# Layer 0 attention: keys on partitions for the probabilities, maxima from a first score product

## The reference, cut to what matters

```
y_dca, y_main = y[:, -DCA:, :], y[:, :-DCA, :]          # DCA = 16
q = _ln((x @ Wq + bq).reshape(b, s1, H, HD), qn_w, qn_b)
k, v             = ... of y_main @ Wk + bk, y_main @ Wv + bv ; k = _ln(k, kn_w, kn_b)
k_dca, v_dca     = ... of y_dca @ Wkv_dca + bkv_dca     ; k_dca = _ln(...)
ctx     = softmax(q k^T * SCALE) v
ctx_dca = softmax(q k_dca^T * SCALE) v_dca
return (ctx + ctx_dca) @ Wo + bo
```

## Time and profile before

| what | us |
|---|---|
| median of three runs | 2358.55 |
| the profiled execution | 2357.19 |
| its span in the trace | 2355.4 |
| projection stage | 7 to 101.6 |
| attention stage | 101.6 to 294.8 |
| output product | 295.0 to 310 |

### The profile page before, as it was taken

One profiled execution on the slowest core, in us unless ns is written; L12 is line 12 of the kernel. 1 busy time (PEld: TensorE's weight loads), 2 busy tenths in 40 slices (PEclk: granted clock), 3 DMA queues, 4 the chain that ended last, 5 costly groups with the idle time before them and its releaser, 6 DMA issues. The chain is left out here.

```text
span 2355.4 us, 42854 instructions
## 1 busy us (share of the span) xinstructions
PE 2082.5 (88%) x12471; PEld 1729.0 (73%) x12471; DVE 1555.0 (66%) x4480; ACT 1226.4 (52%) x3030; POOL 760.3 (32%) x1130
## 2 busy tenths in 40 slices
PE   5698879799999995799999878888769999997999
PEld 3454468577999992588888767777658999986887
DVE  6699857756878884788888752111246877885665
ACT  3799933656666661566666412222216666653333
POOL 3443310202333320323332166666622333311221
PEclk9799989899999997899999888999889999997999
DMA  2157020102211204000000137776750000004331
GB/s 63 37 111 204 1 90 1 67 7 88 74 56 67 73 19 146 5 1 0 0 0 1 45 101 202 212 209 194 210 177 21 21 20 13 20 2 127 110 109 52
DMA packets 132900, 174.04 MB, mean 74 GB/s; under 512 B 43868, under 2 KB 99140, under 8 KB 130088
## 3 DMA queue, kind: packets, MB, share of 16 engines
q1 hardware_dynamic: 121704, 140.27, 20.5%
q0 software_dynamic: 10656, 29.11, 4.0%
q10 hardware_dynamic: 416, 3.15, 0.3%
HBM read 155.57 MB, written 36.83 MB: 82 GB/s over the span
## 5 line engine op out<-in xcount | busy, mean ns | idle before, releaser
L2515 DVE COPY l2f_x_t<-bank 128x256 f32<-128x256 f32 x111 | 46.6, 424 | 267.3 <-remote 123.9
L1259 ACT ACTIVATE l0a_prob<-bank,l0a_shift 128x496 f32<-128x496 f32 (+1 forms) x256 | 161.7, 1169 | 2.3 <-DVE l0a_shift L1283 2.3
L701 ACT ACTIVATE l1a_prob<-l1a_masked,l1a_shift,l1a_q_scale 128x512 f32<-128x512 f32 x128 | 104.5, 816 | 80.1 <-DVE l1a_shift L759 79.0
L2390 POOL DMA_INDIRECT l2f_x_rows_of<-l2f_x_rows,l2f_table x111 | 108.2, 974 | 85.4 <-remote 40.7
L2257 PE MATMUL bank<-l2f_x_t,l2f_w 128*128 128x128 f32 x888 | 129.8, 294 | 6.4 <-issue 5.8
L701 ACT ACTIVATE l2a_prob<-l2a_masked,l2a_shift 128x512 f32<-128x512 f32 x128 | 92.7, 724 | 81.0 <-DVE l2a_shift L763 78.2
L701 ACT ACTIVATE l3a_prob<-l3a_masked,l3a_shift 128x512 f32<-128x512 f32 x128 | 92.7, 724 | 79.3 <-DVE l3a_shift L763 76.6
L2346 ACT ACTIVATE l2f_h<-bank 128x128 f32<-128x128 f32 x111 | 30.8, 278 | 186.9 <-PE bank L2257 89.9
L2257 PEld LDWEIGHTS bank<-l2f_x_t,l2f_w 128*128 128x128 f32 x888 | 119.0, 208 | 10.8 <-issue 10.7
L1259 ACT ACTIVATION_READ_ACCUMULATOR l0a_prob<-bank,l0a_shift 128x1 f32 x256 | 125.4, 900 | 0.0
L2395 POOL DMA_INDIRECT l2f_y_rows<-l2f_y,l2f_target x111 | 110.4, 994 | 38.4 <-issue 33.9
(11 more groups left out here) (590 smaller groups left out, 7491.6 us busy)
## 6 DMA issues: line engine op xcount, KB each, us to landing
l2f_w<-w_rows SPq DMA_DIRECT2D x111, 304.0 KB
l1a_side<-rms SPq DMA_DIRECT2D x16, 1024.0 KB, 4.9
w_rows<-in_l2f_w SPq DMA_DIRECT2D x4, 2048.0 KB
l2f_hots<-l2f_y_rows SPq DMA_DIRECT2D x8, 768.0 KB, 9.9
l3f_raw<-in_l3f_w SPq DMA_DIRECT2D x24, 256.0 KB, 3.8
l3f_mix<-shares SPq DMA_DIRECT2D x16, 384.0 KB, 3.6
l2f_w_rest<-in_l2f_w SPq DMA_DIRECT2D x111, 48.0 KB
w_rows<-in_l2f_w SPq DMA_DIRECT2D x8, 512.0 KB
```

The costliest lines, as they stand in the source:

```text
L701: act.activation(prob[:, unit, :], masked[:, unit, :], ACT.Exp, bias=shift[:, unit:unit + 1], scale=q_scale[:, slot, t:t + 1] if qk_norm e ...
L1259: last = act.activation(prob[:, at, q, first:end], score_bank[at % 2 * 2 + q][:, first:end], ACT.Exp, bias=shift[:, at, q, part:part + 1], ...
L2390: pool.indirect_dma_start(x_rows_of[:, b % of.X_SLOTS, :], None, x_rows, bass.IndirectOffsetOnAxis(table[:, b:b + 1], 0)).then_inc(gathere ...
L2515: dve.tensor_copy(x_t[:, b % 2, :], turn_bank[b % 2][:, 0:D]).then_inc(x_kept, 1)
```

## The change

The attention stage is written anew, and the projection stage prepares for it.

- **First score product, for maxima only.** As before 128 queries by 512 keys; VectorE reduces each bank to 32 maxima of 16 keys (`coarse`), and at the end of a group 31 of them to the maximum of the first 496 keys (`top`); the 32nd is that of the last 16.
- **Maxima as rows.** POOL writes both maxima, each as a high and a low part, into four columns of a zeroed tile `shift`; PE turns it (`shifts`), VectorE adds the turned rows to the queries (`shift_queries`), whose fourth share is zero in these rows. In the keys' fourth share stand -1 or 0, so that the next product has the maximum already taken off.
- **Second score product, keys on partitions.** Per head and half of the keys two products of 128 keys by 256 queries (`turned_scores`); ScalarE takes the exponential of 512 columns straight into `prob_t`. No transposes, no accumulator.
- **Totals from a column of ones.** Values are 17 wide, the 17th being one. Five products per head and quad (a *quad* is four heads, two groups) instead of four: the last key tile twice, with `m.v0` holding zero for the last 16 keys and `m.v0_last` zero for all others, into two halves of the bank.
- **Division at the end.** ScalarE evicts the quad, VectorE spreads each head's row of totals over its 32 partitions (`stream_shuffle`) and takes the reciprocal of all 512 columns, POOL multiplies and adds the two halves into `m.o0`.
- **Projection.** VectorE computes the low part once rather than twice (512 columns, not 1024); ScalarE copies the columns of -1 and 0 into both buffers of `parts` once (steps 4 and 5); the value bias is masked by two kinds of tile, and the last key tile of each batch takes two operations for one; small masks, two memsets and the ones are set on VectorE and POOL at the start.
- The stages are unrolled: 38 steps, one group entering in each of the first 32; queries, keys and values are read where they lie, without staging copies.

```
@@ projection
+                    if s in (query_steps, query_steps + 1):
+                        for j in range(2):
+                            kind = minus[:, int(s % 2 and j), :].rearrange("p (h d) -> p h d", h=1)
+                            act.copy(parts[:, s % 2, j * HEADS:(j + 1) * HEADS, 3, :], kind.broadcast_to([P, HEADS, H0]))
...
+                pool.memset(parts[:, :, :, 3, :].bitcast(F32), 0.0).then_inc(cleared, 1)
...
+                for n, kind in enumerate((is_common, is_last)):
+                    dve.tensor_scalar(bkv_kept[:, n, :]..., bkv[:, 1, :]..., kind[:], None, ALU.mult).then_inc(own, 1)
...
+                            if n < KT - 1:
+                                last = dve.tensor_tensor(m.v0[:, n, of_batch, 0:H0], of, bias, ALU.add)
+                                continue
+                            for to, kind, part in ((m.v0[:, n, of_batch, 0:H0], is_common, 0),
+                                                   (m.v0_last[:, of_batch, 0:H0], is_last, 1)):
+                                last = dve.scalar_tensor_tensor(to, of, kind[:], bkv_kept[:, part, :]..., ALU.mult, ALU.add)
...
-                    dve.tensor_tensor(low, head[...].broadcast_to([P, rows, 2, H0]), high.bitcast(F32), ALU.subtract)
+                    low = 2 if s < query_steps else 1
+                    dve.tensor_tensor(of[:, :, low, :], head[:, s % 4, :, :], of[:, :, 0, :].bitcast(F32), ALU.subtract)
@@ attention, tensor engine
+                def scores(g, u):
+                    n, j, q = 4 * g + u, (u + 1) % 2, u // 2
+                    wait_for(pe, coarse_done, n - 2)
+                    pe.matmul(score_bank[n % 3][:], m.q0_t[rows(j), g, q * P:(q + 1) * P], m.k0_t[rows(j), g, :], ...)
+                def turned_scores(g, u):
+                    n, j, half = 4 * g + u, u % 2, u // 2
+                    if u == 0:
+                        pe.wait_ge(q_shifted, g + 1)
+                    wait_for(pe, exp_done, n - 1)
+                    for key in range(2):
+                        first = (2 * half + key) * P
+                        last = pe.matmul(turned_bank[u % 2][:, key * 2 * P:(key + 1) * 2 * P],
+                                         m.k0_t[rows(j), g, first:first + P], m.q0_t[rows(j), g, :], ...)
+                def shifts(g):
+                    pe.wait_ge(shift_set, g + 1)
+                    for q in range(2):
+                        last = pe.transpose(shift_bank[:, q * P:(q + 1) * P], shift[:, g % 2, q, :].bitcast(F32), m.ident[:])
...
+                for i in steps:                      # range(groups + 6)
+                    for u in range(4):
+                        if is_group(i):
+                            scores(i, u)
+                        if is_group(i - 2):
+                            turned_scores(i - 2, u)
+                        if u == 1 and is_group(i - 1):
+                            shifts(i - 1)
+                        if u > 0 and quad_at(i, 3) is not None:       # even steps
+                            values(quad_at(i, 3), u - 1)
+                        if u < 2 and quad_at(i, 4) is not None:       # odd steps
+                            values(quad_at(i, 4), u + 3)
@@ attention, VectorE
+                def invert(quad):
+                    dve.wait_ge(o_kept, quad + 1)
+                    of = total[:, quad % 2, :, :]
+                    dve.stream_shuffle(of, o_parts[:, quad % 2, :, :], [H0] * V0).then_inc(spread, 1)
+                    dve.wait_ge(spread, quad + 1)
+                    dve.reciprocal(of, of).then_inc(inverse_done, 1)
...
+                for i in steps:
+                    for u in range(4):
+                        if is_group(i):
+                            largest(i, u)            # waits for scores_ready; 512 columns to 32 maxima
+                        if u == 0 and quad_at(i, 5) is not None:      # even steps
+                            invert(quad_at(i, 5))
+                        if u == 2 and is_group(i - 1):
+                            shift_queries(i - 1)     # waits for shift_turned; adds 256 columns to m.q0_t
+                    if is_group(i):
+                        dve.wait_ge(coarse_done, 4 * i + 4)
+                        dve.tensor_reduce(top[:, i % 2, :, :], coarse[:, i % 2, :, :, 0:sixteens - 1], AX_X, ALU.max)
@@ attention, POOL: per group set_shift (waits for top_done: two copies, a wait, two subtractions), per quad add_parts
+                    pool.tensor_tensor(parts, parts, total[:, quad % 2, :, :], ALU.mult).then_inc(scaled, 1)
+                    pool.wait_ge(scaled, quad + 1)
+                    pool.tensor_tensor(m.o0[:, quad, :], parts[:, 0, :], parts[:, 1, :], ALU.add).then_inc(added, 1)
```

More of the change, by code:

```diff
@@ L1069, in biased @@
                             b, n = divmod(i - TT, KT)
[L1070 to L1073, removed]
+                            of_batch = slice(b * HEADS, (b + 1) * HEADS)
+                            of, bias = (a.rearrange("p (h a d) -> p h a d", h=HEADS, a=2)[:, :, 1, :]
+                                        for a in (bank[:], bkv[:, 0, :]))
+                            if n < KT - 1:
[3 more added lines that the diff above has]
+                                                   (m.v0_last[:, of_batch, 0:H0], is_last, 1)):
+                                last = dve.scalar_tensor_tensor(to, of, kind[:], bkv_kept[:, part, :].rearrange(
+                                    "p (h d) -> p h d", h=HEADS), ALU.mult, ALU.add)
                         last.then_inc(v_done, 1)
@@ L1115, in small_attention_stage @@
     scale = float(H0) ** -0.5
[L1116 to L1119, removed]
+    groups, quads = BATCH * GROUPS, BATCH * GROUPS // 2
+    slots = 8
     width = SHARES * H0
+    sixteens = KEYS // LAST_KEYS
     with Stage(nc, m, "l0a") as st:
[L1122 to L1132, removed]
-        o_bank = st.banks("o", 2)
[L1134 to L1156, removed]
-            return not isinstance(pair, int) or 0 <= pair - back < PAIRS
@@ new lines, in small_attention_stage @@
+        coarse = st.sbuf("coarse", [P, 2, GROUP, 2, sixteens])
+        top = st.sbuf("top", [P, 2, GROUP, 2])
+        shift = st.sbuf("shift", [P, 2, 2, P], F32R)
+        prob_t = st.sbuf("prob_t", [P, slots, KT, 2 * P])
+        o_parts = st.sbuf("o_parts", [P, 2, 2, 2 * P])
+        total = st.sbuf("total", [P, 2, 2, 2 * P])
+        score_bank = st.banks("score", 3)
+        turned_bank = st.banks("turned", 2)
+        shift_bank, = st.banks("shift", 1)
+        o_bank = st.banks("o", 2)
@@ L1159, in small_attention_stage, with is_group, quad_at @@
+        def is_group(g):
+            return 0 <= g < groups
+        def quad_at(step, back):
+            quad = (step - back - 1) // 2
+            return quad if (step - back) % 2 and 0 <= quad < quads else None
+        steps = range(groups + 6)
         with st.block() as block:
@@ new lines, in _ @@
+            @block.scalar
+            def _(act):
+                for i in steps:
+                    g = i - 2
+                    for u in range(4):
+                        if is_group(g):
+                            j, half = u % 2, u // 2
+                            if u == 0:
+                                wait_for(act, pv_ready, g // 2 - 1)
+                            act.wait_ge(turned_ready, 4 * g + u + 1)
+                            act.activation(prob_t[:, (2 * g + j) % slots, 2 * half:2 * half + 2, :],
+                                           turned_bank[u % 2][:].rearrange("p (n t) -> p n t", n=2), ACT.Exp,
+                                           scale=scale).then_inc(exp_done, 1)
+                        quad = quad_at(i, 4)
+                        if u == 2 and quad is not None:
+                            act.wait_ge(pv_ready, quad + 1)
+                            wait_for(act, added, quad - 1)
+                            act.copy(o_parts[:, quad % 2, :, :], o_bank[quad % 2][:].rearrange("p (n t) -> p n t", n=2)
+                                     ).then_inc(o_kept, 1)
@@ L1300 @@
+                pool.wait_ge(shift_high, 1)
+                for i in steps:
+                    if is_group(i):
+                        set_shift(i)
+                    if quad_at(i, 5) is not None:
+                        add_parts(quad_at(i, 5))
 class OutputWeights:
```

222 lines of the change are left out of this document (97 added, 125 removed).

## The result

The changed kernel takes **2377.05 us** (median of six runs, 2368.81 to 2385.16) against 2357.23 on the same chip (six runs, 2353.80 to 2361.49): a ratio of **1.008** (95% interval 1.0055 to 1.0105), slower. Forecast were 2367 us, 2345 to 2388, and slower as the likeliest outcome. Its profiled execution lasted 2375.49 us, with a span of 2373.5.

A forecast was written before the change was run, and what follows sets the result against it. ScalarE bounded the old kernel; in the new one the reciprocal and the VectorE, POOL, PE handover would. Attention +7.3, output product +3.4, projection -1.9 make +8.8: 2357.19 becomes 2366.0, median 2367 us, range 2345 to 2388.

The forecast's parts named there:

- VectorE's work: Attention loop, per quad: maxima, reductions, additions, shuffle and reciprocal sum to 10.1 us, against 11.48 before.
- Rival D: Attention loop: unseen VectorE and POOL operations, shuffle and reciprocal among them, are dearer; 2380 us; chance 0.13.
- The handover: Attention loop: VectorE waits through POOL and PE for its third reduction; odd step 4.53, even 7.12, quad 11.65 us.
- Rival B: Odd step's gap mostly absent, VectorE never idle at 10.2 us a quad; 19 us less, 2348; chance 0.27.
- The clock inside the loop: PE's granted clock in the attention loop: assumed full after the head, so no cost there.
- rival C: PE stays at the low clock in the attention loop; quad 14.4 us, 36 us more, 2402; chance 0.10.
- Head and tail: Attention's first steps, 0 to 5, take 30.2 us; its serial end after step 31 takes 18.8.
- Output product: After attention: one low-clock stretch of some 6.8 us at its start, PE doing half; +3.4 us.
- Projection: Stage before attention: less subtraction work, against added bias copies and ScalarE copies; -1.9 us in sum.

The follow-up runs named there:

- the kernel with the halves: The changed kernel with half of the reciprocal moved to the odd step and POOL's scaling one step later; ratio 1.0014 to the kernel before.
- The filled kernel: The changed kernel plus matrix products nobody reads, five ahead of shift products, five ahead of odd steps' first score product, more in the tail; ratio 1.0082.
- the control: The changed kernel as it is, run again on another chip; 2314.39 us against 2301.19 for the kernel before, ratio 1.006.
- the logarithm kernel with three fillers: The changed kernel with ScalarE's logarithm and exponential for the reciprocal, plus unread products on PE, three for each five; ratio 0.9983 to the kernel before.

## Why the prediction was right, and where its size was not

**VectorE's work**: right, 10.1 us a quad predicted and 10.14 measured. Shuffle 0.73 (0.7); reciprocal 3.35 (3.25), and 1.75 for 256 columns in the kernel with the halves: 6.3 ns a column between the two, where the small ones had given 6.0.

```profile
L1294 DVE RECIPROCAL l0a_total<-l0a_total 128x256 f32<-128x256 f32 x16 | 28.1, 1753 | 0.5
```

The estimate that the prediction took from the Trainium skill (VectorE: DVE Perf Modes, "First, the fixed hardware budget"), 4.3 us by its repeat count of 8, is too high; the trace disagrees, as the 64-column row had. Rival D is out. In its even step the prediction put 4.04 us for shuffle and reciprocal where its own prices add up to 3.95; 4.04 is what the trace has (209.98 to 214.02), and for the 0.09 the prediction gave no reason.

**The handover**: right in kind. Odd step 4.27 for 4.53, third reduction 2.41 us after the first for 2.67, VectorE idle 0.98 ahead of it for 1.4; even 7.02 for 7.12. At full clock a quad is 11.29 us, 0.2 less than the 11.48 before, where the forecast had 0.2 more: by itself the loop would have gained 2.5 us. Rival B is out.

**The clock inside the loop**: the step that failed. The prediction had a full clock through the loop (forecast) or a half one (rival C, 14.4 us a quad) and judged by a wait of 0.4 us a pair. It was neither: it toggled, and what counts is where a low stretch falls. Six of the thirteen odd steps from step 7 to 31 were longer, five by 1.0 to 1.1 us and the last by 1.7 (its third reduction comes 4.08 us after the first), +7.1 us; a quad at full clock was 0.36 below its forecast. From step 6 to the end of 31: 153.8 us for 151.5, and 149.2 before. So the loop is slower than before's by the clock, a term that the forecast put at nothing, and not by the longer chain that it had in its place; that its sign came out is luck.

**Head and tail**: head 28.0 for 30.2. Tail 22.7 for 18.8, the term that was most undersized: the low clock lay over most of it (0.57), with the last exponentials 1.7 us apart and the last forty records of value products 3.8 us for 2.9. The filled kernel's 3.4 us less shows that. **Output product**: +2.8 for +3.4, by the low clock at its start as predicted; shown by the fillers. The prediction named no row for its stretch of 6.8 us; the granted clock was low there for some 5.6 us (0.84 over 17.6). **Projection**: -2.5 for -1.9.

Sum for layer 0: attention's length +11.3 for +7.3, output product +2.8 for +3.4, projection -2.5 for -1.9: +11.6 for +8.8 (+9.6 in the control). That is the change's own price. By the figures above the low clock makes up 7.1 us of it in the loop, 3.4 in the tail and 2.8 in the output product, together more than the whole: without it the change would be about even, by this estimate. The rest of the profiled execution's +18 us on the first chip came in layer 2's feed-forward and was not seen in the control. There the medians differ by 13.2 us, and the profiled execution is the fastest of four; what made the others longer, and the stage on the first chip, stays open. Without those 6 us the median would be some 2371, within the range as well.

## What to carry to other kernels

Moving work off the bounding engine pays only what the next chain leaves: write out the new chain with its handovers, and price a reciprocal on VectorE by its columns (6 ns each here), not by its place in a list of cheap operations. Where a change gives PE more or longer waits (29 us of them here for 19), work every step out at both levels of its clock, and look where a low stretch would fall: under another engine's work it was free here, in a chain through PE it was not. Fillers on PE paid here with the long VectorE instruction halved, where the clock then held; they did not with it whole, where the clock still fell and VectorE waited for a product that stood behind them.

## What the runs showed of the hardware

A change of function on ScalarE between exponential and logarithm is a table load of 1.28 us each way, here 32 of them, and nothing stands between a load and the activation behind it (206.26 after 204.97 + 1.28). The exponential of the logarithm needs a load of its own, though the step's other exponentials behind it need none. The Trainium skill (ScalarE: Activation LUTs, "What ACT_TABLE_LOAD costs") has the load at the same 1283 ns and a drain of some 1380 ns with each; the trace shows none: both loads and both activations lie within 3.9 us. The granted clock did not follow PE's busy share alone: with PE busy 127.2 of 146.4 us it was 0.91 in the filled change, and with 127.5 it was 0.99 in the logarithm kernel with three fillers (products at the low clock count as busy for longer, so the two are not quite alike). Which pattern of waits brings it down is not settled by these runs.
